# Softmax pass of a graph network: value minus the last maximum from PE instead of DVE

## What is computed

```python
m = jax.nn.relu(feat[src]) + EPS
logits = BETA * m
seg_max = jax.ops.segment_max(logits, dst, num_segments=N)
ex = jnp.exp(logits - seg_max[dst])
denom = jax.ops.segment_sum(ex, dst, num_segments=N)
a = ex / denom[dst]
msg = jax.ops.segment_sum(a * m, dst, num_segments=N)
feats = feat + msg
return feats @ W + b
```

## Time and profile before

| | us |
|---|---|
| median of 3 runs | 5516.88 |
| lowest and highest | 5506.9 and 5519.22 |
| the profiled execution | 5542.31 |
| its span, first to last instruction | 5540.4 |
| PE busy | 3184.8 (57%) |
| DVE busy | 2663.9 (48%) |
| POOL busy | 2500.9 (45%) |
| ACT busy | 1558.5 (28%) |

### The profile page before, as it was taken

One profiled execution on the slowest core, in us unless ns is written; L12 is line 12 of the kernel. 1 busy time (PEld: TensorE's weight loads), 2 busy tenths in 40 slices (PEclk: granted clock), 3 DMA queues, 4 the chain that ended last, 5 costly groups with the idle time before them and its releaser, 6 DMA issues.

```text
span 5540.4 us, 71225 instructions
## 1 busy us (share of the span) xinstructions
PE 3184.8 (57%) x18737; PEld 2336.6 (42%) x18737; DVE 2663.9 (48%) x5882; ACT 1558.5 (28%) x3677; POOL 2500.9 (45%) x2580
## 2 busy tenths in 40 slices
PE   0444444444465555455545555320117999999999
PEld 0333333333443333333333333210006777778777
DVE  3777777777644444454445554540001144433333
ACT  1666666676222222222222222210000011111000
POOL 6555555555555555555555555677770000000000
PEclk9999999999966666666666666655558999999999
DMA  6555555555223333333333333210005756666776
GB/s 198 173 179 178 172 181 174 175 181 169 66 79 102 102 97 101 98 101 100 100 95 102 102 101 102 73 56 0 0 12 202 269 195 248 247 250 248 256 277 230
DMA packets 418286, 801.74 MB, mean 145 GB/s; under 512 B 237496, under 2 KB 294684, under 8 KB 391980
## 3 DMA queue, kind: packets, MB, share of 16 engines
q1 hardware_dynamic: 270182, 591.99, 31.8%
q0 software_dynamic: 82320, 90.28, 7.8%
q10 hardware_dynamic: 65718, 118.62, 5.7%
HBM read 581.84 MB, written 218.74 MB: 144 GB/s over the span
## 4 chain that ended last, share of the span: by engine, by line
PE 28%; issue 23%; another core or an unknown queue 22%; DVE 12%; ACT 7%; SPq 3%; ACTq 2%; POOL 1%; DMA 1%; DVEq 1%; POOLq 0%
PE ps L1166 16%; PE ps L1096 6%; DVE second L1675 3%; SPq L629 2%; DVE area L1691 2%; ACT ps L1215 2%; DVE second L1685 2%; ACT dump L1219 1%; ACT out_ring L1231 1%; ACT relu_dump L1215 1%; ACT out_ring L1239 1%; ACTq L1241 1%; PE ps L921 1%; PE ps L928 1%
## 5 line engine op out<-in xcount | busy, mean ns | idle before, releaser
L939 PE MATMUL ps<-ident,area 96*128 96x96 f32 x2352 | 435.6, 352 | 1083.8 <-ACT out_ring L1231 416.3
L779 POOL DMA_INDIRECT area<-src_table,idx_src x784 | 751.0, 958 | 510.2 <-DMA idx_src<-src_dram 261.0
L779 POOL DMA_INDIRECT area<-relu_table,idx_src x784 | 740.4, 944 | 533.4 <-issue 324.8
L939 PEld LDWEIGHTS ps<-ident,area 96*128 96x128 f32 x2352 | 347.0, 210 | 1208.1 <-issue 855.6
L1662 DVE TENSOR_TENSOR_SCAN area<-flags,area,ps 96x512 f32<-96x512 int8 x196 | 249.7, 1274 | 960.5 <-ACT dump L1219 743.0
L1166 PE MATMUL ps<-second,area 128*128 128x288 bf16 x5194 | 650.7, 286 | 0.2 <-DVE second L1809 0.2
L1166 PEld LDWEIGHTS ps<-second,area 128*128 128x128 f16 x5194 | 508.3, 98 | 127.6 <-DVE second L1809 0.5
L1627 DVE SCALAR_TENSOR_TENSOR second<-second,area,ps 128x512 bf16<-128x512 f32 x784 | 538.5, 743 | 0.0
L788 POOL DMA_INDIRECT adj<-copies_ring,cell_ring x392 | 389.0, 992 | 326.2 <-DVE cell_ring L1643 206.4
L921 PE MATMUL ps<-second,w_ef_scaled 96*96 96x512 f32 x392 | 313.2, 893 | 288.2 <-ACT second L1263 173.9
L1096 PE MATMUL ps<-early,area 128*128 128x288 bf16 x2401 | 328.5, 293 | 259.6 <-issue 259.6
(11 more groups left out here) (330 smaller groups left out, 4657.5 us busy)
## 6 DMA issues: line engine op xcount, KB each, us to landing
area<-adj SPq DMA_DIRECT2D x147, 1632.0 KB
area<-adj SPq DMA_DIRECT2D x55, 1568.0 KB
adj<-early SPq DMA_DIRECT2D x102, 816.0 KB
soft_sums<-out_ring ACTq DMA_DIRECT2D x196, 384.0 KB
second<-key_dram SPq DMA_DIRECT2D x98, 512.0 KB
area<-dst_table SPq DMA_DIRECT2D x784, 48.0 KB
sums<-out_ring ACTq DMA_DIRECT2D x196, 192.0 KB
second<-caps_dram SPq DMA_DIRECT2D x98, 192.0 KB
```

Source lines behind the costliest of these rows:

```text
L779: pool.indirect_dma_start(out=src_rows[:, s, c, :], out_offset=None, in_=gather_table[p], in_offset=bass.IndirectOffsetOnAxis(ap=idx_src[s ...
L939: last = nc.tensor.transpose(ps[:, b, c * F:(c + 1) * F], r[:, (s * CH + c) * P:(s * CH + c + 1) * P], ident[0:F, 0:F])
```

## The change

In the softmax pass PE makes value minus last maximum in PSUM. A new step rise follows turn and project of each tile. It turns the gathered rows a second time, with four ordinary fp32 matmuls against the identity, into bank 4 + s % 2, and then, when maxed(t) has come, adds a 96x512 matmul of last_max with diag_s, which now holds minus one on its diagonal. That last matmul counts scored. DVE's subtraction is gone. ACT reads the difference from PSUM for both branches and makes sank before rose, since rose overwrites the bank. POOL's gather waits for scored(t - 4) in this pass, because rise reads src_rows too. turn_back and copy_back run one tile later than before (two_before), with two of each behind the loop. PE waits for index_made before the pass, and DVE fills diag_s once at the start. rise waits for summed(t - 2), the last reader of its bank.

```diff
@@ -439,6 +439,13 @@
+        def two_before(step, u, s):
+
+            if s >= 2:
+                step(u, s - 2)
+            elif not isinstance(u, int) or u:
+                step(u - 1, RING + s - 2)
@@ -772,7 +779,7 @@
-                    wait(pool, e["turned"], t - RING + 1)
+                    wait(pool, e["scored"] if kind == SOFT else e["turned"], t - RING + 1)
@@ -929,6 +936,17 @@
+                def rise(u, s):
+                    t = u * RING + s
+
+                    wait(pe, e["summed"], t - 1)
+                    for c in range(CH):
+                        nc.tensor.matmul(ps[0:F, DECAY_BANK + s % 2, c * P:(c + 1) * P], src_rows[:, s, c, :], ident[:, :],
+                                         start=c == 0, stop=False)
+                    wait(pe, e["maxed"], t + 1)
+                    nc.tensor.matmul(bank(DECAY_BANK + s % 2, F), diag_s[:, :], last_max[:, s * TE:(s + 1) * TE],
+                                     start=False, stop=True).then_inc(e["scored"], 1)
+
@@ -943,14 +961,17 @@
                 def turn_and_project(u, s):
                     turn(u, s)
                     project(u, s)
+                    rise(u, s)
...
                 if kind == SOFT:
-                    over_tiles(pe, turn_and_project, lambda u, s: tile_before(turn_back, u, s))
-                    turn_back(EI - 1, RING - 1)
+                    pe.wait_ge(index_made, 1)
+                    over_tiles(pe, turn_and_project, lambda u, s: two_before(turn_back, u, s))
+                    for s in (RING - 2, RING - 1):
+                        turn_back(EI - 1, s)
@@ -1247,13 +1268,13 @@
                     wait(act, e["scored"], t + 1)
-                    rise, rose, sank = weight[:, s % 2, :], bank(DECAY_BANK + s % 2, F), weight[:, s % 2, :]
-                    nc.scalar.activation(rose, rise, ACT.Relu).then_inc(e["parted"], 1)
+                    rose, sank = bank(DECAY_BANK + s % 2, F), weight[:, s % 2, :]
+                    nc.scalar.activation(sank, rose, ACT.Relu, scale=-1.0).then_inc(e["parted"], 1)
                     act.wait_ge(e["parted"], 2 * t + 1)
-                    nc.scalar.activation(sank, rise, ACT.Relu, scale=-1.0).then_inc(e["parted"], 1)
-                    nc.scalar.activation(rose, rose, ACT.Exp, scale=-1.0)
+                    nc.scalar.activation(rose, rose, ACT.Relu).then_inc(e["parted"], 1)
+                    nc.scalar.activation(sank, sank, ACT.Exp, scale=-1.0)
                     act.wait_ge(e["parted"], 2 * t + 2)
-                    nc.scalar.activation(sank, sank, ACT.Exp, scale=-1.0).then_inc(e["expd"], 1)
+                    nc.scalar.activation(rose, rose, ACT.Exp, scale=-1.0).then_inc(e["expd"], 1)
@@ -1272,8 +1293,9 @@
                 if kind == SOFT:
-                    over_tiles(act, soften, lambda u, s: tile_before(copy_back, u, s))
-                    copy_back(EI - 1, RING - 1)
+                    over_tiles(act, soften, lambda u, s: two_before(copy_back, u, s))
+                    for s in (RING - 2, RING - 1):
+                        copy_back(EI - 1, s)
@@ -1452,6 +1474,7 @@
+            v.tensor_scalar(diag_s[:, :], ident[0:F, 0:F], -1.0, None, ALU.mult)
@@ -1676,8 +1699,6 @@
                     dve.wait_ge(e["maxed"], t + 1)
-                    v.tensor_tensor(weight[:, b, :], bank(b, F), last_max[:, s * TE:(s + 1) * TE], ALU.subtract)\
-                     .then_inc(e["scored"], 1)
```

## The result

The changed kernel takes 5453.14 us (median of 5, 5444.23 to 5477.91); the kernel before, beside it, 5516.34. The ratio is 0.990, with a 95% interval of 0.988 to 0.992: **63 us faster**. The profiled execution of the changed kernel took 5477.91 us, its slowest, with a span of 5475.8; that of before had 5542.31 and 5540.4. The 64.6 us between the spans are found again in the softmax pass.

A forecast was written before the change was run, and what follows sets the result against it. POOL's gather runs, stopped by late PE counts, were taken to pace the softmax pass; 6.60 against 6.44 us a tile gave +31, plus +3, so 5516.9 + 34 = 5551, said as 5550 us; range 5425 to 5665.

The forecast's parts named there:

- What bounds the pass: Softmax pass: PE's counts are held late in POOL's gather runs until POOL stops; POOL with two waits sets 6.5 us a tile.
- POOL stops after two tiles, and the index wait is gone: POOL's softmax gathers: runs become 8 gathers long, indices arrive in time; 12.9 us for two tiles, 6.45 a tile.
- The stop, 4.19 us: POOL's step from a run's last gather to the next run's first, held by a PE count: 4.19 us.
- PE's 6.6: PE in the softmax pass: 6.4 to 6.9 us a tile at the lower clock, taken as 6.6: +31 us.
- the +3 of the forecast: Pass start and end: later turn_back about 2 us at the end, one more DVE instruction at the start; +3 us in all.
- DVE's subtraction at 0: Dropping DVE's subtraction in the softmax pass, 120 us of work, lies beside POOL's cycle with DVE partly idle: 0 gain.
- two held counts in a row: Slower rival: POOL stops for a scored whose turned is itself held; 7.15 us a tile, +142, 5659 us; chance 0.16.
- The stricter gate: POOL's gather of tile t waits for scored(t-4), not turned(t-4): 2.3 to 3.3 us later where it binds.
- The later turn_back: Softmax pass on PE: costs nothing inside, since out_ring has 4 slots, and about 2 us at the pass's end.
- PE at 2.4 GHz for the whole pass: Faster rival: PE needs 3.3 us a tile and is out of the way; 6.2 a tile, 5473 us; chance 0.13.
- Three tiles a cycle: Faster rival: the second scored gets through before POOL stops; 6.0 us a tile, 5430 us; chance 0.12.
- The signs named for a faster outcome: Softmax pass: projections of 413 ns throughout, runs staying at 12 gathers, or scored never late, each pointing to a faster rival.

The follow-up runs named there:

- sub_held: Changed kernel with DVE's subtraction done again in vain behind the maximum scan, PE's counts late: 5677.40 us beside 5577.04 for the kernel before, ratio 1.0178.
- all_but_rise: Kernel before plus POOL's wait for scored and the later turn_back and copy_back, subtraction still on DVE, counts late: 5546.45 us beside 5513.93, ratio 1.0076.

## Why the prediction was wrong

Forecast: 5550 us, slower; measured: 5453, faster. By its own steps:

- **What bounds the pass** was read rightly: late counts of PE behind POOL's runs. The runs with counts in time showed how much: 6.44 us a tile fall to 5.3. That the wait would be there in some sessions only, the forecast did not know; its own session had it. The stretch was drawn too short: the text has counts held from about 9 us into a run, and in before 35 of the 39 counts made 5 to 6 us into a run of eight or more are late already.
- **POOL stops after two tiles, and the index wait is gone**: right, 89 of 101 runs, and in POOL's waits from 400 to 1320 us the index loads come to 3.4 us in all.
- **The stop, 4.19 us, failed: it is 3.44.** It was taken from the earlier trace rows, the stop behind twelve gathers, and put behind eight. Behind eight, counts are let go 1.72 us after the run, behind twelve 2.35. So two tiles are 7 x 1.25 + 3.44 = 12.2 us and a tile 6.10, not 6.45: 0.35 x 196 = 69 us. The text had named 6.2 "if the wait at the stop shrinks", and had the rows of before, with runs of 4, 8 and 12, to measure it by.
- **PE's 6.6, on top of that, failed**: PE had the upper level in 7 tiles of 10, was busy 4.6 us a tile (302 / 65), and was hidden. 0.15 x 196 = 29 us. Both terms together are 98 us, and 5551 - 98 = 5453. That this meets the measurement to the microsecond is luck: the tile measured 6.14, not 6.10, which is 8 us more, and some 9 us less came from outside the pass and from the +3 of the forecast. The first and the last scan are 1198 us apart, where the text expected some 1290.
- **DVE's subtraction at 0** held only in the sum. It was argued from idle time, and sub_held shows that the cycle the forecast counted on exists only without the subtraction: with it, 7.10 a tile, close to the slow rival, "two held counts in a row", put at 7.15. That rival had the stop right, 4.19 + 2.8 = 7.0 against 6.98 in 42 runs, and gave it to the wrong kernel; that the tile agrees too is in part luck, since the rival has none of the 49 runs of four gathers.
- **The stricter gate**: together with the order part a loss, as all_but_rise shows, through the scan and the subtraction behind a held turning. By itself it met late counts in no run. **The later turn_back** costs nothing, as said; **scored is held too**, 79 of 159 late.
- **PE at 2.4 GHz for the whole pass** (5473) came nearest by time, with 0.7 of its condition. **Three tiles a cycle** didn't come: one run in a hundred has twelve gathers.
- The signs named for a faster outcome did appear in part: projections of 413 ns, in most tiles. PE over 70% busy was right. Nothing outside the pass moved by more than 4.4 us.

What stays open: what decides whether counts are late, what exactly is queued, and whether the recording takes part. How 0.69 us of DVE work tips the cycle is read from one stop, not proved for all of them, and what part the clock has in the gain is not separated. The 63 us themselves hold for sessions with late counts; without them no part of the change is worth more than 4 us.

## What to carry to other kernels

When a cycle is built of runs and stops, measure the stop as a function of the run's length before moving it to a shorter run. Idle time of an engine says that it isn't full, not that its work is free: what counts is whether its result lands ahead of the point in the cycle at which others stop waiting in time. And look at the same kernel in several sessions before building on a wait that no instruction explains, and at whether the trace has all its semaphore events: here the wait was worth 990 of 5516 us, came and went, and came only with gaps in the record.

## What the runs showed of the hardware

PE's counts came more than 8 us late in the softmax pass while POOL issued gathers in a row (8.4 for turned in before), in some sessions and in others not at all (at most 0.02 us), on the same chips, with equal durations of the scan and the turning. Of the other engines' recorded counts in the pass three are late in before, all of DVE in its first two tiles, and none in the changed kernel. The late ones were let go 1.2 us after a run of four gathers and some 0.15 us later for each further one. A fill of 128x1 on POOL with a wait for it costs 0.90 us between two gathers, of which the fill is 0.11. Turning four 128x96 blocks by transposes leaves PE at 658 ns a projection; eight ordinary products a tile more brought 145 of 196 down to 413.
